# Reordering the start, the third slot and the last slots of a two-layer graph attention kernel

## The reference

```python
h = relu(layernorm(x))
# layer 0: 8 heads of 64
m = h @ map_w.T + map_b
n = m per head / its norm;   cos = n @ n.T, 0 where masked
q, k = m @ q_w.T + q_b, m @ k_w.T + k_b
p = softmax(q @ k.T / 8, masked) * keep
a = (cos > 0.1) * p
x = x + relu((a @ (h @ gcn_map_w.T + gcn_map_b)) @ gcn_W.T / (a.sum(-1) + 1))
# layer 1: 4 heads of 64
h = relu(layernorm(x))
p = softmax((h @ Wq) @ (h @ Wk).T / 8, masked)
x = x + (p @ (h @ Wv)) @ Wo + bo
```

## Time and profile before

| what | value |
|---|---|
| runs (3) | median 2530.55 us, 2529.49 to 2531.10 |
| the profiled execution | 2531.93 us, span 2530.10 us |
| TensorE busy | 2487.9 us, 98% of the span |
| VectorE, ScalarE, GpSimd busy | 79%, 67%, 83% |
| granted TensorE clock, mean | 0.997 |
| instructions | 78433 |

### The profile page before, as it was taken

The page is one execution under the profiler, slowest core; times in us unless marked ns, Lnnn a source line. Parts: engine busy times, 40 slices in busy tenths (PEclk is TensorE's granted clock), DMA queues, the critical chain, the costliest instruction groups (busy, mean ns, idle before and its releaser), DMA issues.

```text
span 2530.1 us, 78433 instructions
## 1 busy us (share of the span) xinstructions
PE 2487.9 (98%) x30472; PEld 1994.3 (79%) x30472; DVE 1989.3 (79%) x3483; ACT 1687.7 (67%) x4456; POOL 2104.0 (83%) x2393
## 2 busy tenths in 40 slices
PE   7899999999999999999999999999999999999997
PEld 6787877877878878878778778788788788787775
DVE  6878788777778788787787877787787877878875
ACT  5666676676676676666666766766766766667665
POOL 4898888888888888888888888888888888888884
PEclk9999999999999999999999999999999999999999
DMA  5565666566666665656665665665556556656544
GB/s 152 98 121 112 123 121 116 117 121 118 116 119 117 122 117 115 125 114 122 124 114 119 125 114 117 118 119 119 118 117 125 114 119 125 113 121 125 115 91 92
DMA packets 826450, 298.01 MB, mean 118 GB/s; under 512 B 768352, under 2 KB 776032, under 8 KB 826080
## 3 DMA queue, kind: packets, MB, share of 16 engines
q1 hardware_dynamic: 826080, 292.99, 59.1%
HBM read 75.80 MB, written 33.55 MB: 43 GB/s over the span
## 4 chain that ended last, share of the span: by engine, by line
PE 93%; DVE 2%; ACT 1%; POOL 1%; issue 1%; DMA 1%; SPq 0%; POOLq 0%; DVEq 0%; ACTq 0%
PE unit_ps L1838 26%; PE unit_ps L2011 26%; PE unit_ps L1852 25%; PE s_ps L1862 4%; PE s_ps L1919 4%; PE c_ps L1862 3%; PE unit_ps L1983 2%; PE unit_ps L1862 2%; PE unit_ps L1930 1%; PE c_ps L1895 1%; ACT e_ec L930 0%; DVE e_ec L1245 0%; DMA e_ec<-in_L_gnn_q_w_dram 0%; DMA sq_rest<-sq_t 0%; POOL e_ec L714 0%
## 5 line engine op out<-in xcount | busy, mean ns | idle before, releaser
L930 ACT ACTIVATE e_ec<-e_ec,neg_mx 128x128 f32<-128x128 f32 x1016 | 392.9, 388 | 4.2
L2011 PE MATMUL unit_ps<-m_hl,w_q_hi 128*128 128x256 f16 x2048 | 356.6, 273 | 0.0
L2011 PE MATMUL unit_ps<-m_hl,w_k_hi 128*128 128x256 f16 x2048 | 355.6, 272 | 0.4 <-DVE qk_sb L1281 0.4
L1021 ACT ACTIVATE qk_hl<-qk_sb 128x512 f16<-128x512 f32 x256 | 153.5, 623 | 287.1 <-DVE qk_sb L1281 287.1
L1838 PE MATMUL unit_ps<-h_t,w_m_hi 128*128 128x256 f16 x2048 | 339.6, 273 | 2.2 <-DVE qk_sb L1281 1.2
L1852 PE MATMUL unit_ps<-w_v_hi,h_t 128*128 128x512 f16 x1024 | 325.1, 379 | 0.0
L709 POOL TENSOR_TENSOR p_hl<-p_sb,p_hl 128x512 f16<-128x512 f32 x128 | 148.6, 1161 | 169.8 <-ACT p_hl L951 169.8
L1838 PE MATMUL unit_ps<-h_t,w_m_lo 128*128 128x256 f16 x1024 | 279.2, 273 | 0.0
L714 POOL TENSOR_TENSOR e_ec<-e_ec 128x1024 f16<-128x1024 f32 x127 | 270.7, 2132 | 7.2 <-ACT e_ec L958 7.2
L2011 PE MATMUL unit_ps<-m_hl,w_q_lo 128*128 128x256 f16 x1024 | 237.5, 273 | 0.0
L2011 PE MATMUL unit_ps<-m_hl,w_k_lo 128*128 128x256 f16 x1024 | 237.3, 272 | 0.0
(11 more groups left out here) (264 smaller groups left out, 7583.3 us busy)
## 6 DMA issues: line engine op xcount, KB each, us to landing
xa<-in_x_dram SPq DMA_DIRECT2D x128, 256.0 KB, 3.5
xres<-in_x_dram SPq DMA_DIRECT2D x128, 256.0 KB, 2.8
out_dram<-ybuf SPq DMA_DIRECT2D x128, 256.0 KB, 2.4
h_t<-h_hl SPq DMA_TRANSPOSE x255, 3.2
ec_t<-e_ec SPq DMA_TRANSPOSE x254, 3.2
adj_in<-in_adj_dram SPq DMA_DIRECT2D x128, 16.0 KB, 2.4
p_t<-p_hl SPq DMA_TRANSPOSE x126, 3.3
o_t<-o_hl SPq DMA_TRANSPOSE x126, 3.5
```

Of the source, the lines that this page charges most:

```text
L930: ins = nc.scalar.activation(e[:, h, :], e[:, h, :], ACT.Exp, bias=neg[:, h:h + 1], scale=SCALE, accum_out=sums[:, h:h + 1])
L1021: nc.scalar.activation(dst[:, 0, c, :], src[:, c, :], ACT.Copy).then_inc(done, 1)
L2011: ins = nc.tensor.matmul(ps[:, c % 2 * 2 * P:(c % 2 + 1) * 2 * P], w[a][:, i, c * P:(c + 1) * P], parts[:, b, i, :], start=n == 0, stop=n ...
```

## The change

It has three parts.

1. **Preparation.** `gather_top` and `spread_top` of q move behind q's turns on TensorE; ScalarE splits v's weights before it squares q's, and makes m's upper part before the squares of k; VectorE's `peaks("top_q")` moves behind the lower parts of v's weights.
2. **Third slot.** VectorE's list of slot 2 becomes a function of its own, with `attended`, `x1_stats`, `gate` and `square_rest` ahead of the two weights.
3. **Last slots.** Graph 126 gets its own buffer for exponentials (`e_before`, in `xa`), so its mask waits for `h_lo` and not for `e_lower` of graph 125. The o1 parts of the last two graphs go to `h_hl`, their results to `h1_sb` (`y_of`, semaphore `y_late`). The o1 of the last four graphs is turned on TensorE (`turn_last_o1` 0 to 3) and no longer by DMA for 124 and 125. `lq` of z moves between `k01` and `k23`, `lk` of z in front of `weighted_sums(a)`, and the lists of all engines change to go with it.

```diff
-    (-3, "q01"), (-3, "o1e"), (-3, "q23"), (-3, "o1o"), (-3, "norm"), (-3, "k01"), (-3, "k23"), (-3, "nt"), (-3, "wo"),
-    (-1, "last_a"), (-1, "last_b"), (-3, "lq"), (-3, "lk"), (-2, "lv"), (-2, "s1a"), (-2, "s1b"), (-2, "wo"), (-1, "lq"), (-1, "lk"),
+    (-3, "q01"), (-3, "o1e"), (-3, "q23"), (-3, "o1o"), (-3, "norm"), (-3, "k01"), (-3, "lq"), (-3, "k23"), (-3, "nt"), (-3, "wo"),
+    (-1, "last_a"), (-1, "last_b"), (-3, "lk"), (-2, "lv"), (-2, "s1a"), (-2, "s1b"), (-2, "wo"), (-1, "lq"), (-1, "lk"),
...
+        e_before = xa[:, :, :].rearrange("p a d -> p (a d)").rearrange("p (h n) -> p h n", h=H)
+        def o1_parts(g):
+            return h_hl[:, g % 2, :, 0:INNER] if g >= B - 2 else o_hl[:, g % 2]
+        def y_of(s):
+            return h1_sb[:, s.n - 5 - (B - 2), :] if s.n - 5 >= B - 2 else ybuf[:, s.n % 2, :]
         def e_of(s):
-            return e_last if s.n == B - 1 else e_sb
+            return e_last if s.n == B - 1 else e_before if s.n == B - 2 else e_sb
...
 # SP
             store(z)
+            load_residual(b)
             turn_e(a, 0, e_hi)
+            turn_e(b, 0, e_hi)
             turn_e(a, 1, e_lo)
-            load_residual(b)
-            turn_e(b, 0, e_hi)
             turn_e(b, 1, e_lo)
...
-            turn_o1(d)
-            turn_o1(e)
...
 # GpSimd
+            def result_base_late(s):
+                pool.wait_ge(h1_lo, B)
+                nc.gpsimd.tensor_tensor(y_of(s), x1[:, (s.n - 5) % 8, :], bias_o[:, :], ALU.add).then_inc(y_late, 1)
...
             p1_lower(e, 4)
+            o1_lower(d, 5)
             p1_lower(e, 3)
-            o1_lower(d, 5)
             o1_lower(d, 4)
-            result_base(d)
+            result_base_late(f)
+            result_base_late(g)
             o1_lower(f, 5)
             o1_lower(f, 4)
+            result_base(d)
             result_base(e)
-            result_base(f)
-            result_base(g)
...
 # ScalarE, preparation
             squares_of(st_gcn, GM, w_v[0][:, :, :])
+            act.wait_ge(square_sum, 1)
+            for c in range(C):
+                split_upper("make_v", w_v, c, V, 2)
             for c in range(C):
                 act.wait_ge(q_in[c], 16)
             squares_of(st_q, QW, w_q[0][:, :, :])
-            act.wait_ge(square_sum, 1)
-            for c in range(C):
-                split_upper("make_v", w_v, c, V, 2)
+            m_upper(early)
             act.wait_ge(k_in, 16)
             squares_of(st_k, KW, w_k[0][:, :, :])
-            m_upper(early)
...
 # ScalarE, last slots
             scores_exp(a)
-            lqk_upper(z, "lq", lq_hl, LQ)
+            scores_exp(b)
             e_upper(a)
-            scores_exp(b)
             lqk_upper(z, "lk", lk_hl, LK)
             e_upper(b)
...
             l1_exp(c, 4)
+            lqk_upper(d, "lq", lq_hl, LQ)
+            lqk_upper(d, "lk", lk_hl, LK)
+            o1_upper(b, 5)
             l1_exp(c, 3)
-            o1_upper(b, 5)
-            lqk_upper(d, "lq", lq_hl, LQ)
             o1_upper(b, 4)
-            lqk_upper(d, "lk", lk_hl, LK)
+            lv_upper(e)
             l1_exp(e, 4)
             l1_exp(e, 3)
-            lv_upper(e)
...
 # VectorE, the mask of a graph
-                    wait(dve, e_lo, s.at(lambda t: t if t != B - 1 else t - 1))
+                    if s.n < B - 2:
+                        wait(dve, e_lo, s.at(lambda t: t))
+                    elif s.n == B - 2:
+                        dve.wait_ge(h_lo, B)
...
+            def third_slot(s):
+                attended(s)
+                x1_stats(s)
+                gate(s)
+                square_rest(s)
+                l1_weights_lower(2)
+                v_features(s, "va", 0)
+                l1_weights_lower(3)
+                x_stats(s)
+                v_features(s, "vb", 1)
...
 # VectorE, last slots
             scores_mask(a)
-            result(z)
             scores_mask(b)
             gate(a)
+            result(z)
             attended(a)
             x1_stats(a)
-            lqk_lower(z, "lq", lq_hl, LQ, 0)
             gate(b)
             lqk_lower(z, "lk", lk_hl, LK, 1)
...
             lqk_lower(d, "lq", lq_hl, LQ, 0)
+            lqk_lower(d, "lk", lk_hl, LK, 1)
             o1_rows(b, 4)
-            lqk_lower(d, "lk", lk_hl, LK, 1)
...
 # TensorE, preparation
             feature_chunk(ps, w_m, 2, 0, h)
-            pe.wait_ge(square_sum, 2)
-            gather_top("top_q", QW, 1)
             feature_chunk(ps, w_m, 3, 1, h).then_inc(unit_full, 1)
-            spread_top("top_q", 1, 2)
             ps = start_prep("bias_v")
...
             for c in (3, 0, 1, 2):
                 turn("turn_q", st_q, c)
+            pe.wait_ge(square_sum, 2)
+            gather_top("top_q", QW, 1)
+            spread_top("top_q", 1, 2)
             evicted("make_v")
...
 # TensorE, last slots
             qk_part(z, "k", w_k, 0)
+            lqk_part(z, "lq", w_lq)
             qk_part(z, "k", w_k, 1)
             turn_norms(z)
             output(z)
             scores(a)
             cosines(a)
             scores(b)
+            lqk_part(z, "lk", w_lk)
             weighted_sums(a)
-            lqk_part(z, "lq", w_lq)
-            lqk_part(z, "lk", w_lk)
             cosines(b)
             l1_values(a)
             l1_scores(a)
...
             l1_scores(e)
+            l1_values(e)
             output(b)
-            l1_values(e)
             l1_sums(d, 5)
+            turn_last_p1(0)
             l1_sums(d, 4)
             output(c)
-            turn_last_p1(0)
             turn_last_p1(1)
+            turn_last_o1(0)
             l1_sums(f, 5)
             l1_sums(f, 4)
+            turn_last_o1(1)
             output(d)
-            turn_last_o1(0)
+            turn_last_o1(2)
+            turn_last_o1(3)
             output(e)
-            turn_last_o1(1)
             output(f)
             output(g)
```

More of the change, by code:

```diff
@@ L361, in build @@
         p1_kept = [sem(f"p1_kept{i}") for i in range(2)]
-        o1_turned = [sem(f"o1_turned{i}") for i in range(2)]
-        o1_kept = [sem(f"o1_kept{i}") for i in range(2)]
+        o1_turned = [sem(f"o1_turned{i}") for i in range(4)]
+        o1_kept = [sem(f"o1_kept{i}") for i in range(4)]
+        y_late = sem("y_late")
         et_in = sem("et_in")
@@ L443, in build @@
         PREP = ([("turn_m", c) for c in range(C)] + [("turn_gcn", 0), ("top_m", 0), ("top_m", 1)]
-                + [("make_v", c) for c in range(C)] + [("top_v", 0), ("top_v", 1), ("top_q", 0), ("top_q", 1), ("bias_v", 0)]
-                + [("turn_q", c) for c in (3, 0, 1, 2)] + [("top_k", 0), ("top_k", 1)] + [("turn_k", c) for c in (3, 0, 1, 2)]
+                + [("make_v", c) for c in range(C)] + [("top_v", 0), ("top_v", 1), ("bias_v", 0)]
+                + [("turn_q", c) for c in (3, 0, 1, 2)] + [("top_q", 0), ("top_q", 1)] + [("top_k", 0), ("top_k", 1)] + [("turn_k", c) for c in (3, 0, 1, 2)]
                 + [("top_l", 0), ("top_l", 1)])
@@ L559, in store @@
                     settle(sp, settled_sp, s.i)
-                    sp.dma_start(out[s.graph(-5)], ybuf[:, s.n % 2, :]).then_inc(y_out[s.n % 2], 16)
+                    sp.dma_start(out[s.graph(-5)], y_of(s)).then_inc(y_out[s.n % 2], 16)
             def turn_x(s):
@@ L702, in o1_lower @@
                     b = (s.n - behind) % 2
-                    nc.gpsimd.tensor_tensor(o_hl[:, b, 1, :], o1_sb[:, b, :], o_hl[:, b, 0, :], ALU.subtract).then_inc(o1_lo, 1)
+                    parts = o1_parts(s.n - behind)
+                    nc.gpsimd.tensor_tensor(parts[:, 1, :], o1_sb[:, b, :], parts[:, 0, :], ALU.subtract).then_inc(o1_lo, 1)
             def p1_lower(s, behind):
@@ L1011, in o1_upper @@
                     b = (s.n - behind) % 2
-                    wait(act, o1_in[b], s.at(lambda t: 16 * ((t - behind) // 2)))
-                    nc.scalar.activation(o_hl[:, b, 0, :], o1_sb[:, b, :], ACT.Copy).then_inc(o1_hi, 1)
+                    if s.n - behind >= B - 2:
+                        act.wait_ge(h_in, 16 * B)
+                    else:
+                        wait(act, o1_in[b], s.at(lambda t: 16 * ((t - behind) // 2)))
+                    nc.scalar.activation(o1_parts(s.n - behind)[:, 0, :], o1_sb[:, b, :], ACT.Copy).then_inc(o1_hi, 1)
             def qk_upper(s, name, src, dst, half, done):
@@ L1463, in slot @@
                 scores_mask(s)
+                if s.n == 2:
+                    third_slot(s)
+                    return
                 if s.odd:
@@ L1681, in _ @@
             m_features(early, 1)
+            peaks("top_q", 1, 2)
             scale_q()
@@ L1762, in _ @@
             l1_max(e, 3)
+            lv_lower(e)
             result(b)
-            lv_lower(e)
             o1_rows(d, 5)
+            p1_keep(0)
             o1_rows(d, 4)
             result(c)
-            p1_keep(0)
             p1_keep(1)
+            o1_keep(0)
             o1_rows(f, 5)
             o1_rows(f, 4)
+            o1_keep(1)
             result(d)
-            o1_keep(0)
```

(13 more changed lines are left out.)

50 lines of the change are left out of this document (27 added, 23 removed), and 2 rows, old and new, of the table LATE_UNITS.

## The result

The changed kernel is slower: 2535.66 us in the median of 21 runs (2531.28 to 2537.32) against 2532.57 (2529.49 to 2535.87) for the kernel before in the same session. The ratio is 1.0013, with a 95% interval of 1.0007 to 1.0018, so +3.3 us (+1.8 to +4.6). That is under the 0.2% named in the prediction, and outside its range (2523.5 to 2532.0).

A forecast was written before the change was run, and what follows sets the result against it. TensorE, busy 98% of the span, was taken as the bound. Terms -1.9 - 0.3 + 3.0 + 0.4 - 3.45 = -2.25 us, from the runs' median 2530.55, gave 2528.3 us; range 2523.5 to 2532.0.

The forecast's parts named there:

- Preparation, -1.9: Start of the kernel: the new order brings `q01` to 32.85 instead of 34.75, gaining 1.9 us (bounds 1.3 and 2.3).
- Third slot, -0.3: Slot 2's new list removes the 2.45 us wait at `scores(3)`, but only 0.3 us is kept.
- the stall went where the prediction sent it: Third slot: the stall moves to the mask's reader, the next `weighted_sums`, and to `norms(3)`, starting at 104.4 to 105.2.
- The price of the two weights: Third slot: the first weight meets GpSimd's `e_lower` (2.2 us), the second finds GpSimd idle (1.3 us).
- Middle, +3.4: Tail up to the last graph's x1: a loss of 3.0 us from lateness plus 0.4 for half clock.
- The slip to `attended(c)`: Tail: `attended(c)` begins near 88.0 instead of 84.94, 3.0 us late (bounds 1.9 and 3.6).
- the two orders named in the prediction: Tail: ScalarE has `scores_exp(b)` ahead of `e_upper(a)`; SP has `turn_e(b,0)` ahead of `turn_e(a,1)`, delaying `weighted_sums(b)`.
- I take 0.4 for it: Tail: possible half clock after TensorE idles some 3 us before `turn_last_h1`, up to 1.7 us, entered as 0.4.
- End, -3.45: Tail's end: last `l1_scores` 3.15 us earlier plus 0.3 by the last result, gain 3.45 us (bounds 2.0 and 5.0).
- B: Rival: the tail's middle does not slip and the end keeps its 3.45; -5.65 us, 2524.9; chance 0.22.
- C: Rival: the third slot keeps its whole 2.45 us, the rest as forecast; 2526.1 us; chance 0.08.
- D: Rival: slower, half clock from `weighted_sums(b)` through `lq`, `lk`, `lv` of b and c; +3.4 us, 2533.9; chance 0.10.

The follow-up runs named there:

- head_both: Kernel before with the new preparation and the new third slot, old tail; ratio 0.9998 (0.9989 to 1.0007).
- prep_alone: Kernel before with the new order of the preparation only; ratio 1.0002 (0.9993 to 1.0011).
- no_third: Kernel before with the new preparation and the new end, third slot and tail's middle as before; ratio 0.9981 (0.9973 to 0.9990), -4.8 us.
- end_alone: Kernel before with only the tail's changes behind `attended(c)`; ratio 0.9985 (0.9976 to 0.9994), -3.8 us.
- after_again: The changed kernel, unchanged, measured a second time; ratio to the kernel before 1.0009 (1.0000 to 1.0018).
- fill_norms: Changed kernel with 8 extra matmuls in front of `norms(3)` in slot 3; ratio to the kernel before 1.0008 (0.9999 to 1.0016).
- third_alone: Kernel before with the new third slot only; ratio 1.0000 (0.9991 to 1.0009).
- exp_b_back: Changed kernel with `e_upper(a)` again ahead of `scores_exp(b)` and `turn_e(a,1)` ahead of `turn_e(b,0)`; ratio to the kernel before 0.9989 (0.9981 to 0.9998), -2.8 us.
- middle_back: Changed kernel with the tail's middle as before; preparation, third slot and end new; ratio to the kernel before 0.9984 (0.9975 to 0.9992), -4.1 us.
- best_old_third: Kernel before with new preparation and end, plus extra matmuls before `m(0)`, `weighted_sums(a)` and `turn_last_h1`; ratio 0.9984 (0.9975 to 0.9993), -4.1 us.
- best_new_third: Kernel before with new preparation, third slot and end, extra matmuls before `m(0)`, `norms(3)`, `weighted_sums(a)`, `turn_last_h1`; ratio 0.9978 (0.9969 to 0.9987), -5.6 us.
- fill_best: Changed kernel with the old middle and extra matmuls before `m(0)`, at two slot 3 waits, before `weighted_sums(a)`, `turn_last_h1`; ratio to the kernel before 0.9990, -2.5 us.

## Why the prediction was wrong

Its sum was -1.9 - 0.3 + 3.0 + 0.4 - 3.45 = -2.25. Measured: +0.2 + 0.9 + 5.1 - 3.2 = +3.0. The end was right. Three steps failed, and they have a root in common: terms were taken from one execution, and half clock was priced in the tail only.

**Preparation, -1.9: the step "`q01` starts at 32.85 instead of 34.75" failed as a mean.** At full clock the arithmetic holds to the hundredth: `head_both`, whose `m01` starts at 17.18, has `q01` at 32.86. But in the new order this is a chain: `q01` starts 15.68 us behind `m01` in 7 of the 10 profiles, and `m01` started anywhere from 17.1 to 18.3 in them. In the old order the squares of q, that is the landing of q, hold `q01` at 34.13 to 34.75 whenever `m01` comes. The profile that I worked from had `m01` at the early end (17.14), so the gain of 1.9 was nearly the best case. The mean is 1.1: `m01` at 17.79 in those ten, 15.68 more is 33.47, and the old order's `q01` is at 34.57.

Then the half clock: `m01` in 3 profiles of 10 (never in 4 with the old order), 1.4 us longer each, and `m(0)` in 8 of 10 (1 of 4), 1.7 us longer each. Together with the 1.1 this makes the table's +0.2, but the records speak against putting it down to the new order. `m01` runs before the two orders part: the first 91 matmuls in TensorE's record (up to 21.4 us in the kernel before), the first 11 instructions in ScalarE's and the first 50 in VectorE's are the same in both. And in front of `m(0)` both have the same waits (0.35, 0.92 and 1.0 us); from `q01` to the first scores it takes 21.5 us without half clock in `m(0)` and 23.1 with it, in either order. Extra matmuls in the last of these waits kept the clock up in 4 profiles of 4, so the half clock belongs to them as far as so few can tell; that the new order met it more often may be chance. So what the profiles show is a term of 1.1 instead of 1.9. The timed runs can't tell it from nothing: `prep_alone` has +0.5 (-1.8 to +2.8), and `no_third`, which is `end_alone` with the new preparation, is 1.0 us under it by ratios whose intervals overlap.

**Third slot, -0.3: the stall went where the prediction sent it; the step that failed is that nothing else follows.** Both waits came as named (1.67 and 1.91 us), and `norms(3)` came no earlier. The price of the two weights fell on the other one than I wrote: the first started 0.13 us before GpSimd's `e_lower` and took its 1.28 us, `e_lower` took 3.14 us instead of 2.13, and the second weight, started while it still ran, took 2.49 us. VectorE and GpSimd in the changed kernel:

```profile
95.74 1.28 DVE L1685 SCALAR_TENSOR_TENSOR w_lk_lo<-x,scale,w_lk_hi 128x1024 f16<-128x1024 f32 x1
95.87 3.14 POOL L725 TENSOR_TENSOR e_ec<-e_ec 128x1024 f16<-128x1024 f32 x1 [1.98 <-ACT e_ec L969]
97.60 2.49 DVE L1685 SCALAR_TENSOR_TENSOR w_lv_lo<-p_sb,scale,w_lv_hi 128x1024 f16<-128x1024 f32 x1
```

The Trainium skill (SBUF — State Buffer, "Who interferes with whom") has such instructions exclude each other, and the one that comes first is not held up; the trace agrees in all seven profiles. But two waits of 3.6 us together, with 0.9 us of work between, bring the half clock: in all 7 profiles with the new slot and no extra matmuls in it, TensorE is at 0.50 somewhere between 102 and 113 us, in the 7 with the old one never (in four of those it is at half clock between 94 and 101 us, and slots 0 to 4 take 77.6 us all the same: the wait of 1.14 us at `norms(3)` is gone in these four, so it takes the loss up). How long the clock stays down decides the loss. TensorE in the changed kernel and in `after_again`, from 101 to 113 us:

```profile
101.00:113.00 12.00, 8.42 (x101) 0.86 0.54 103
```

```profile
101.00:113.00 12.00, 8.42 (x87) 0.72 0.56 105
```

The mean clock there is 0.86 in two of the seven (`changed`, `head_both`), and they lose nothing (77.63 and 77.64 us); it is 0.72 in the other five, and they lose 1.1 to 1.4. That gives 0.9 in the mean. `fill_norms` had one profile without that loss and no gain in time, and `third_alone` ran at 1.0000, so the size of this term rests on the profiles, not on a timed run.

**Middle, +3.4: the mechanism was right, the term was too small, it was 5.1.** The slip to `attended(c)` is 3.16 us by the two profiles (3.0 forecast), and `exp_b_back` shows that the two orders named in the prediction are the cause. Missing are 1.7 us. One part is the term "I take 0.4 for it": behind `turn_last_h1` the clock fell in 3 profiles of 5, at least 1.7 us each, so 1.0, which is 0.6 more. Another 0.9 is that the profile before was itself a dear case of the old tail: its `turn_last_h1` comes 41.8 us behind `k01(z)`, in the four others with the old tail 39.8 to 41.6 (mean of the five 41.0). The slip's own 0.16 is the rest. This is also the one term that timed pairs bear out: in the same session `exp_b_back` lies 5 us and `middle_back` 6 us under `after_again`, with intervals that don't touch.

**End, -3.45: right**, -3.2 in the profiles and -3.8 (-6.1 to -1.5) timed alone.

**Rivals.** B (the middle does not slip) and C (the third slot keeps 2.45 us) are out: the slip and the moved stall are in every profile. D was the one on the right side, at +3.4 us, and is no hit for that: TensorE was at half clock from the wait on, but `lq` of b, which starts at 2488.02 in the first profile, is at half clock for its first 0.7 us only and `lk` not at all; the loss is spread over up to five places of the kernel, and that its size came out like D's is luck. It is the same root though, a stall that costs once as idle time and once as half clock behind it.

The Trainium skill (TensorE: Matmul & The Clock Gate, "What's actually happening") adds that the watch over TensorE's activity runs freely and is not started by the kernel, so that one kernel can meet the half clock in one run and not in another. The trace agrees: `before` and `end_alone` have the same instructions in the first 120 us, both wait 1.0 us in front of `m(0)`, and it takes 5.41 us in the one and 7.08 in the other. Put beside the waits in the head, this would have been a term with a chance of its own, the same for both orders.

**A version that beats both.** Of the six kernels with the new end and without the middle's slip, five are 0.15 to 0.22% under the kernel before: `end_alone`, `no_third`, `middle_back`, `best_old_third`, `best_new_third` (-5.6 us, the lowest); the sixth is `fill_best`, 0.10% under it. Their intervals overlap, so which of them is best stays open; against the changed kernel the five save 6 to 9 us by the ratios.
